# Routed experts of a Perceiver block: blocks of 64 places in pairs, weights of the fixed blocks loaded ahead

## The chip, the cores and the metric

The kernel runs on one core of a Trainium2 chip. The metric is the device time of one execution in microseconds (us). The core has TensorE (PE in the profile, with its weight loads as PEld), VectorE (DVE), ScalarE (ACT), GpSimd (POOL) and SyncE (SP), and 16 DMA engines that all queues share. SBUF has 128 partitions. PSUM has 8 banks of 512 f32 words per partition.

## The reference, cut to what matters

Six residual sub-layers follow one another on 8 x 64 = 512 tokens of width 256. Five are untouched in what they compute: cross attention, a delta-rule memory, a dense sum of 8 gated experts, a grouped cross attention, and a self attention (called stage e below). The sixth is a mixture of experts in which each token takes one expert:

```python
def _L1_ffn_ref(x, Wr, br, W1, b1, W2, b2):
    xf = x.reshape(-1, D)                       # 512 tokens x 256, already layer-normed
    logits = xf @ Wr.T + br                     # 8 experts
    expert_idx = jnp.argmax(logits, axis=-1)
    h = relu(einsum('td,efd->etf', xf, W1) + b1[:, None, :])      # 1024 wide
    y = einsum('etf,edf->etd', h, W2) + b2[:, None, :]
    out = y[expert_idx, arange(512)]
```

How many tokens an expert gets is known only at run time.

## The kernel before, in words

Each engine has its own program, written out by hand. They meet at semaphores only. The order of the work on an engine is the order of its lines.

**Router.** After stage e, `xn_tok` holds the normed tokens (partition = token). PE turns them round (`tr_pe`), waits for the two small arrays of the router (`in_wrt`, `wrt` and `b2f`, which SP loads at L474 to L476 once `x_tok` is complete), and makes the logits (L1057). DVE finds the first maximum and a one-hot `oh8` (L1790 to L1797). PE counts, with matrices of ones, the rank of each token within its expert and the total of each expert (L1065 to L1068). DVE then computes how many blocks each expert needs, where they begin (`starts`), which expert owns each block (`owner`, as row numbers `rows` of the weight array `wf`) and the `place` of each token (L1802 to L1821). In the meantime PE runs matmuls that nobody reads (`warm`, L334).

**Blocks of 128 places.** An expert with n tokens gets ceil(n / 128) blocks, and with 512 tokens and 8 experts there are at most NB = 11. All 11 are always run. For block k:

- *gather* (L1082): 16 one-pass matmuls with the one-hot `pick` (made by DVE, L1825) bring the tokens of the block into PSUM, features on partitions. ACT copies them to `xg` (L1394).
- *up* (L1104): 8 chunks of W1 x 2 halves of the width, each 128x128 weights against 128 places, full f32. The trace shows each such f32 matmul as two instructions, so 32 of them.
- ACT adds the bias and the relu for chunks 0 to 3 (L1408), DVE for chunks 4 to 7 (L1845).
- *down* (L1115): 8 matmuls (16 instructions) of `hb` against the 256 columns of W2, into bank 5.
- ACT and DVE split the result in a high and a low part (`yb_h` L1399, `yb_l` L1836), and *scatter* (L1093) adds it to the tokens in banks 6 and 7 with 8 matmuls against the one-hot `pickT` (L1830).

PE's order in step k is: up(k), scatter(k-1), gather(k+1), down(k). Steps 0 to 2, 9 and 10 are written out, 3 to 8 run in a loop of 3 steps.

**Weights.** One block needs 4104 words per partition, 2.1 MB (`ROW1`). POOL fetches them for every block by index, after `rows` is known (L574), into three buffers used in turn. The fetch for block k waits for down(k-3).

**SP's queue** holds all the direct loads in one order. Before the router come `wqkv` and `wproj` for stage e, then SP waits for `x_tok` and loads `wrt` and `b2f`.

Of the kernel before, what the change touches and what calls it, by code (L numbers as in the profile page):

```python
# [21 lines left out]
NB = NT + NEXP - 1  # L22
# [10 lines left out]
def const_layout():  # L33
# [18 lines left out]
        "column": np.broadcast_to(c, (P, P)),  # L52
        "row": p,
        "full": np.broadcast_to(P * np.arange(NT), (P, NT)),
        "before": np.broadcast_to((P * (c8.T > c8)).reshape(1, -1), (P, NEXP * NEXP)),
        "upto": np.broadcast_to((P * (c8.T >= c8)).reshape(1, -1), (P, NEXP * NEXP)),
        "block": np.broadcast_to(P * np.arange(NB), (P, NB)),
        "slot": p + P * np.arange(NB),
    }
# [63 lines left out]
def perceiver(nc, A, out):  # L123
# [13 lines left out]
    xn_tok = sb("xn_tok", NT, D)  # L137
    y_tok = sb("y_tok", NT, D)
    tmp_tok = sb("tmp_tok", NT, D)
    xnT = sb("xnT", KC, TOK)  # L140
    aT = sb("aT", KC, TOK)
# [4 lines left out]

    xnT_h = nc.alloc_sbuf_tensor("xnT_h", [P, KC, TOK], F32R)
    xnT_l = nc.alloc_sbuf_tensor("xnT_l", [P, KC, TOK], F32R)
# [112 lines left out]
    Ze = ce(NT, H, S)  # L261
    PT = ce(NT, H // 2, P)
    mxe, rie = ce(NT, H), ce(KC, TOK)
    assert ce.at <= after_wo1
    ce = Carve(after_wo1)
    wqkv, wproj = ce(KC, 3 * D), ce(KC, D)
    ce.at = after_wo1 + 2 * KC * FF
    vpair = ce(B, H // 2, 2, DK)
    assert ce.at <= after_ub

    cf = Carve()
    wblk = cf(3, ROW1)
    wf1 = [wblk[:, j, 0:KC * FF].rearrange("p (k n) -> p k n", k=KC) for j in range(3)]
    wf2 = [wblk[:, j, KC * FF:KC * FF + FC * D].rearrange("p (k n) -> p k n", k=FC) for j in range(3)]
    bf1 = [wblk[:, j, KC * FF + FC * D:] for j in range(3)]
# [3 lines left out]
    ohT8 = cf(TOK)  # L279
    over, blocks8 = cf(NEXP, NT), cf(NEXP)  # L280
    ends3, ends, starts3, starts = cf(NEXP, NEXP), cf(NEXP), cf(NEXP, NEXP), cf(NEXP)
    ended, owner, owner_row = cf(NB, NEXP), cf(NB), cf(NB)
    place3, place = cf(NT, NEXP), cf(NT)
    rel_place = cf(NB, NT)
    placed = cf(NT, P)
    placeT = cf(TOK)
    xg = cf(KC, P)
    hb = cf(FC, P)
    xn_h, xn_l = carve_r(cf, "xn_h", NT, D), carve_r(cf, "xn_l", NT, D)
    pick = carve_r(cf, "pick", 3, NT, P)  # L290
    pickT = carve_r(cf, "pickT", 3, TOK)
    yb_h, yb_l = carve_r(cf, "yb_h", D), carve_r(cf, "yb_l", D)
    rows = nc.alloc_sbuf_tensor_at("rows", [P, NB], mybir.dt.int32, offset=arena_base + 4 * cf.at)
    cf(NB)
# [100 lines left out]
    with nc.Block() as block:  # L395
# [3 lines left out]
        def _(sp):  # L399
# [73 lines left out]
            w_in(wproj, A["wproj"], "in_wqkv")  # L473
            sp.wait_ge(sem("x_tok"), 5)  # L474
# [8 lines left out]
        def _(pool):  # L483
# [72 lines left out]
            pool.memset(vpair, 0.0).then_inc(sem("e_set"), 1)  # L556
# [13 lines left out]
            pool.wait_ge(sem("f_rows"), 1)  # L570
            for k in range(NB):
                if k >= 3:
                    pool.wait_ge(sem("f_dn"), k - 2)
                pool.indirect_dma_start(wblk[:, k % 3, :], None, A["wf"],  # L574
                                        bass.IndirectOffsetOnAxis(ap=rows[:, k:k + 1], axis=0))\
                    .then_inc(sem(f"f_w{k % 3}"), 16)
# [3 lines left out]
        def _(pe):  # L580
# [429 lines left out]
            def weighted(t):  # L1010
# [8 lines left out]
                for kc in range(KC):  # L1019
                    for b2 in range(2):  # L1020
                        b = 2 * t + b2
                        for j in range(4):
                            last = pe.matmul(PS[32 * j:32 * j + 32, 2 * (t // 2), at(kc) + b2 * S:at(kc) + (b2 + 1) * S],
                                             vpair[:, b, 4 * kc + j].rearrange("p h d -> p (h d)"),
                                             PT[:, t, 2 * j + kc, b2 * S:(b2 + 1) * S], start=True, stop=True)
# [35 lines left out]
            pe.wait_ge(sem("f_oh8"), 1)  # L1061
# [11 lines left out]
            last.then_inc(sem("f_oht"), 1)  # L1073
            warm(pe, 7, 10)

            def gather(k, j):

                pe.wait_ge(sem("f_pick"), k + 1)
                for kc in range(KC):
                    for t in range(NT):  # L1080
                        for part in (xn_h, xn_l):
                            last = pe.matmul(PS[:, 0, kc * P:(kc + 1) * P], part[:, t, kc * P:(kc + 1) * P],  # L1082
                                             pick[:, j, t, :], start=t == 0 and part is xn_h,
                                             stop=t == NT - 1 and part is xn_l)
                last.then_inc(sem("f_x"), 1)

            def scatter(k, j, last_block=False):

                pe.wait_ge(sem("f_yl"), k + 1)
                pe.wait_ge(sem("f_pickT"), k + 1)  # L1090
                for t in range(NT):
                    for part in (yb_h, yb_l):
                        last = pe.matmul(PS[:, 6 + t // 2, (t % 2) * D:(t % 2 + 1) * D],  # L1093
                                         pickT[:, j, t * P:(t + 1) * P], part[:], start=False,
                                         stop=last_block and t % 2 == 1 and part is yb_l)
                return last

            def step(i, j, first=False, last_step=False):
                k = i * 3 + j
                pe.wait_ge(sem(f"f_w{j}"), i * 16 + 16)  # L1100
                pe.wait_ge(sem("f_xg"), k + 1)
                for c in range(FC):
                    for ki in range(KC):
                        last = pe.matmul(PS[:, 1 + c // 4, (c % 4) * P:(c % 4 + 1) * P],  # L1104
                                         wf1[j][:, ki, c * P:(c + 1) * P], xg[:, ki, :],
                                         start=ki == 0, stop=ki == KC - 1)
                    if c % 4 == 3:
                        last.then_inc(sem("f_upd" if c // 4 else "f_upa"), 1)
                if not first:
                    scatter(k - 1, (j + 2) % 3)  # L1110
                if not last_step:
                    gather(k + 1, (j + 1) % 3)
                for c in range(FC):
                    pe.wait_ge(sem("f_hd" if c // 4 else "f_ha"), k * 4 + c % 4 + 1)
                    last = pe.matmul(PS[:, 5, 0:D], hb[:, c, :], wf2[j][:, c, :], start=c == 0, stop=c == FC - 1)  # L1115
                last.then_inc(sem("f_dn"), 1)

            pe.wait_ge(sem("f_xnl"), 1)
            gather(0, 0)
            pe.wait_ge(sem("f_placed"), 1)  # L1120
            pe.matmul(bank(4), C("ones"), placed.rearrange("p a b -> p (a b)"), start=True, stop=True)\
              .then_inc(sem("f_place"), 1)
            pe.wait_ge(sem("f_ohs"), 1)
# [3 lines left out]
            step(0, 0, first=True)  # L1127
            step(0, 1)
            step(0, 2)
            with pe.Fori(1, NB // 3) as i:  # L1130
                for j in range(3):
                    step(i, j)
            step(NB // 3, 0)
            step(NB // 3, 1, last_step=True)
            scatter(NB - 1, 1, last_block=True).then_inc(sem("f_done"), 1)
# [3 lines left out]
        def _(act):  # L1139
# [220 lines left out]
            act.wait_ge(sem("e_set"), 1)  # L1360
            for n in range(2):
                act.wait_ge(sem("e_v"), n + 1)
                act.copy(vpair[0:S, 4 * n:4 * n + 4, :, 0, :],
# [6 lines left out]
            def turned(t):  # L1370
# [16 lines left out]
            act.copy(xn_h[:].rearrange("p a b -> p (a b)"), xn_tok[:].rearrange("p a b -> p (a b)"))\  # L1387
               .then_inc(sem("f_xnh"), 1)
            act.wait_ge(sem("f_oht"), 1)
            act.copy(ohT8[0:NEXP], PS[0:NEXP, 3, :]).then_inc(sem("f_ohs"), 1)  # L1390

            def tokens(k):
# [528 lines left out]
```

## Time and profile before

| | us |
|---|---|
| median of 3 runs | 948.43 (943.84 to 950.6) |
| the profiled execution's own time | 948.45 |
| its span on the core | 946.6 |
| start of the logits (L1057) | 816.20 |
| start of up(0) (L1104) | 833.20 |
| one block, start of up to start of the next up | 9.77 |
| split of the last result (L1399) | 939.82 |

The span counts from the first to the last instruction of the core. The routed part begins with the logits and ends with the store of the output at the end of the span. The page of the profile gives engine shares over the whole span, so what a change in this part is worth has to be read from the rows of this part.

### The profile page before, as it was taken

How to read it: one execution, taken by the hardware profiler on the slowest of the kernel's cores; microseconds unless marked ns; L12 is line 12 of the kernel's file. 1: busy time of each engine (PE TensorE's matmuls, PEld its weight loads, DVE VectorE, ACT ScalarE, POOL GpSimd, SP SyncE). 2: the span in 40 equal slices, each digit the busy share in tenths (PEclk: the TensorE clock that was granted, in tenths of full speed). 3: DMA queues.
4: the chain of work that ended last, by engine and by line, in shares of the span. 5: the costliest groups of instructions: out<-in, count | busy, mean ns of one | idle time of the engine just before them, and what ended most of it. 6: DMA issues, size and time to landing. Idle time of an engine off the chain costs nothing.

```text
span 946.6 us, 19810 instructions
## 1 busy us (share of the span) xinstructions
PE 886.3 (94%) x7764; PEld 748.1 (79%) x7764; DVE 513.6 (54%) x1168; ACT 414.6 (44%) x814; POOL 109.6 (12%) x105
## 2 busy tenths in 40 slices
PE   5998999999798899999999999999899997989997
PEld 3887887878666888888888888873799566789997
DVE  4776887777617555555555555543465246622322
ACT  3765666656622125444444444424466315111111
POOL 2323332130000700000000000000110012101000
PEclk9999999999999899999999999999899998999999
DMA  8544665454450000330331130054267000175650
GB/s 305 188 161 153 217 222 189 162 186 141 158 221 1 4 3 1 134 134 1 134 134 62 71 133 0 0 190 165 75 240 262 2 1 2 38 317 190 238 197 23
DMA packets 25286, 119.58 MB, mean 126 GB/s; under 512 B 2296, under 2 KB 8208, under 8 KB 21648
## 3 DMA queue, kind: packets, MB, share of 16 engines
q1 hardware_dynamic: 23472, 94.63, 27.2%
q0 software_dynamic: 1760, 24.17, 6.7%
q8 instruction: 41, 0.67, 0.3%
q14 instruction: 13, 0.11, 0.0%
HBM read 118.27 MB, written 0.52 MB: 125 GB/s over the span
## 4 chain that ended last, share of the span: by engine, by line
PE 80%; DVE 8%; DMA 6%; issue 2%; ACT 2%; SPq 1%; POOL 0%; DVEq 0%; ACTq 0%
PE PS L368 12%; PE PS L369 12%; PE PS L370 12%; DMA arena<-in_bias 4%; PE PS L1104 4%; PE PS L1115 4%; PE PS L377 4%; PE PS L664 4%; PE PS L906 3%; PE PS L787 3%; PE PS L925 3%; PE PS L653 2%; PE PS L676 2%; PE PS L1082 2%; PE PS L894 2%
## 5 line engine op out<-in xcount | busy, mean ns | idle before, releaser
L1646 DVE TENSOR_TENSOR w_l<-arena,w_h 128x768 fp32r<-128x768 f32 x64 | 61.2, 957 | 91.6 <-ACT w_h L1276 91.6
L1276 ACT CAST w_h<-arena 128x768 fp32r<-128x768 f32 x64 | 53.4, 836 | 129.2 <-PE PS L370 129.2
L368 PE MATMUL PS<-xnT_h,w_h 128*128 128x512 f32 x256 | 100.5, 393 | 0.8 <-DVE xnT_l L362 0.8
L369 PE MATMUL PS<-xnT_l,w_h 128*128 128x512 f32 x256 | 100.4, 392 | 0.0
L1484 DVE CUSTOM_DVE_ANT_0 arena<-PS,arena 128x512 f32<-128x512 f32 x128 | 87.0, 715 | 24.0 <-PE PS L653 17.9
L370 PE MATMUL PS<-xnT_h,w_l 128*128 128x512 f32 x256 | 99.6, 389 | 0.0
L1176 ACT ACTIVATE arena<-arena 128x1024 f32<-128x1024 f32 x64 | 73.5, 1150 | 11.1 <-DVE arena L1484 11.0
L370 PE MATMUL PS<-w_h,h_l 128*128 128x256 f32 x256 | 72.4, 283 | 0.0
L369 PE MATMUL PS<-w_l,h_h 128*128 128x256 f32 x256 | 72.4, 283 | 0.0
L368 PE MATMUL PS<-w_h,h_h 128*128 128x256 f32 x256 | 72.1, 282 | 0.0
L664 PE MATMUL PS<-consts,arena 128*128 128x128 f32 x512 | 69.1, 279 | 0.7 <-ACT arena L1181 0.4
L664 PEld LDWEIGHTS PS<-consts,arena 128*128 128x128 f32 x512 | 56.6, 142 | 10.9 <-issue 4.2
L1653 DVE TENSOR_TENSOR arena<-PS,arena 128x512 f32<-128x512 f32 x64 | 44.3, 692 | 30.5 <-PE PS L370 28.7
L370 PEld LDWEIGHTS PS<-xnT_h,w_l 128*128 128x128 f32 x256 | 48.1, 188 | 10.4
L368 PEld LDWEIGHTS PS<-xnT_h,w_h 128*128 128x128 f32 x256 | 48.3, 189 | 9.6 <-DVE xnT_l L362 1.2
L369 PEld LDWEIGHTS PS<-xnT_l,w_h 128*128 128x128 f32 x256 | 48.3, 189 | 7.7
L1491 DVE COPY arena<-PS 128x512 f32<-128x512 f32 x64 | 44.0, 687 | 17.0 <-PE PS L664 14.6
L1181 ACT COPY arena<-PS 128x512 f32<-128x512 f32 x64 | 37.2, 584 | 31.6 <-PE PS L664 31.6
L368 PEld LDWEIGHTS PS<-w_h,h_h 128*128 128x128 f32 x256 | 48.9, 191 | 2.4
L369 PEld LDWEIGHTS PS<-w_l,h_h 128*128 128x128 f32 x256 | 48.9, 191 | 2.4
L370 PEld LDWEIGHTS PS<-w_h,h_l 128*128 128x128 f32 x256 | 48.9, 191 | 0.0
L544 POOL COPY tmp_tok<-arena 128x1024 f32 (+1 forms) x4 | 4.2, 1042 | 359.8 <-ACT arena L1313 338.3
(284 smaller groups left out, 1943.1 us busy)
## 6 DMA issues: line engine op xcount, KB each, us to landing
arena<-in_bias SPq DMA_DIRECT2D x64, 512.0 KB, 4.7
arena<-in_wall SPq DMA_DIRECT2D x8, 3072.0 KB, 10.2
hT<-in_ctxT SPq DMA_DIRECT2D x12, 1024.0 KB, 6.8
arena<-in_ctxT SPq DMA_DIRECT2D x4, 1024.0 KB, 6.4
arena<-in_ctxG SPq DMA_DIRECT2D x4, 1024.0 KB, 4.9
hT<-in_ctxG SPq DMA_DIRECT2D x4, 1024.0 KB, 5.5
arena<-in_w SPq DMA_DIRECT2D x2, 1024.0 KB, 6.3
vecs<-in_vecs POOLq DMA_DIRECT2D x1, 1024.0 KB, 5.1
```

Source lines behind the costliest of these rows:

```text
L368: pe.matmul(out, a[0], b[0], start=start, stop=False)
L369: pe.matmul(out, a[0], b[1], start=False, stop=False)
L370: return pe.matmul(out, a[1], b[0], start=False, stop=stop)
L377: last = pe.matmul(PS[:, b0 + t // 2, (t % 2) * D:(t % 2) * D + n], lhsT[:, k, t * P:(t + 1) * P], rhs[:, k, 0:n], start=k == 0, stop=k == ...
L664: last = pe.transpose(PS[:, n, c * P:(c + 1) * P], ring[:, u, (4 * g + c) * P:(4 * g + c + 1) * P], C("ident"))
L1104: last = pe.matmul(PS[:, 1 + c // 4, (c % 4) * P:(c % 4 + 1) * P], wf1[j][:, ki, c * P:(c + 1) * P], xg[:, ki, :], start=ki == 0, stop=ki ...
L1176: act.activation(ring[:, u, :], ring[:, u, :], ACT.Exp, bias=nmax0[:, 1, u:u + 1], scale=-1.0, accum_out=rsum0[:, u:u + 1]).then_inc(sem(" ...
L1276: act.copy(w_h[:, s % 4, :], stage[s // 8 % 2][:, s % 8, :]).then_inc(sem("c_wh"), 1)
L1484: dve.tensor_tensor_reduce(out=ring[:, u, c], in0=bank(j), in1=ring[:, u, c], scale=-1.0, scalar=nmax0[:, 0, u:u + 1] if half else 3e38, o ...
L1491: dve.tensor_copy(pT[:, u % 4, 0:4, :].rearrange("p a b -> p (a b)"), bank(tile_bank("T", u, 0)))\
L1646: dve.tensor_tensor(w_l[:, s % 4, :], stage[s // 8 % 2][:, s % 8, :], wide(w_h[:, s % 4, :]), ALU.subtract).then_inc(sem("c_wl"), 1)
L1653: dve.tensor_tensor(hm[:, s % 2, :], bank(2 + s % 2), sg[:, s % 2, :], ALU.mult)\
```

## The change

**Blocks of 64 places.** Every expert gets one fixed block of 64 places. The tokens of rank 64 and above go to overflow blocks of 64. Seven of these suffice (`OVER`), and all seven are always run. Blocks are taken in pairs: pairs 0 to 3 are the fixed blocks (experts 0 and 1, 2 and 3, ...), pairs 4 to 6 are overflow blocks 0 to 5, and pair 7 is overflow block 6 alone. So there are 8 passes over PE in place of 11.

**PE per pair.** up has, for each of the two blocks, chunks x width halves x *two column halves of 64 weights*, each against 64 places: 64 matmuls, 128 instructions in the trace's count. down has 8 chunks x 2 blocks, 64 weights against 256 columns, where block 0 writes PSUM partitions 0 to 63 and block 1 writes 64 to 127. One scatter serves both blocks. One gather of 256 places serves two pairs, so there are 4 in place of 11.

**DVE and ACT per pair.** 8 relu instructions of 64 places each on either engine, where there were 4 of 128. The router's chain on DVE is reordered: the place of a token in a fixed block needs only its rank, so `picks(0)` and `picks(1)` are made ahead of the counting of overflow blocks. They are now 1024 words wide in place of 512. Five `warm` pairs replace ten.

**Weights.** SP loads the 8 fixed blocks ahead, each with a home of its own in SBUF. The overflow blocks are still fetched by index by POOL, one pair after each of the first four downs. To make room, buffers of stage e move (`Ze` to `hT`, `rie` to `tmp_tok`, `vpair` to `xnT_h` and `xnT_l` in two parts, with two memsets).

**Constants** grow from 1485 to 1617 words per partition.

On SP, at the end of the program, stood (names: out <- in, shape):

```order
L404 DMA arena<-in_wqkv 128x2x768 [waits d_u1,d_u0]
L404 DMA arena<-in_wproj 128x2x256
L404 DMA arena<-in_wrt 128x2x8 [waits x_tok]
L476 DMA arena<-in_b2f 8x256
L478 DMA out<-x_tok 128x4x256 [waits x_tok]
```

and now:

```order
L423 DMA arena<-in_wqkv 128x2x768 [waits d_u1,d_u0]
L423 DMA arena<-in_wproj 128x2x256
L495 DMA arena<-in_wf 128x4104 [waits d_w]
L495 DMA arena<-in_wf 128x4104 x2
L495 DMA arena<-in_wf 128x4104 [waits d_o]
L495 DMA arena<-in_wf 128x4104
L495 DMA arena<-in_wf 128x4104 [waits d_out]
L495 DMA arena<-in_wf 128x4104 [waits e_out]
L495 DMA arena<-in_wf 128x4104
L423 DMA arena<-in_wrt 128x2x8 [waits x_tok]
L510 DMA arena<-in_b2f 8x256
L512 DMA out<-x_tok 128x4x256 [waits x_tok]
```

Eight loads of 2.1 MB stand ahead of `wrt` and `b2f`, the last two of them released by the same stage (`e_out`) that completes `x_tok`.

On PE, the next to last step stood as

```order
L1104 MATMUL PS<-arena 128x128 [waits f_xg,f_w0]
L1104 MATMUL PS<-arena 128x128 x15
L1093 MATMUL PS<-yb_h,pickT 128x256 [waits f_pickT,f_yl]
L1093 MATMUL PS<-yb_l,pickT 128x256
...
L1082 MATMUL PS<-pick,xn_h 128x128 [waits f_pick]
...
L1115 MATMUL PS<-arena 128x256 [waits f_ha] x4
L1115 MATMUL PS<-arena 128x256 [waits f_hd] x4
```

and a pair without a gather now stands as

```order
L1142 MATMUL PS<-hT,arena 64x64 [waits f_xg,f_o2]
L1142 MATMUL PS<-hT,arena 64x64 x63
L1127 MATMUL PS<-yb_h,pickT 128x256 [waits f_pickT,f_yl]
L1127 MATMUL PS<-yb_l,pickT 128x256
...
L1154 MATMUL PS<-arena,hT 64x256 [waits f_ha]
L1154 MATMUL PS<-arena,hT 64x256
```

where the shapes are those of the output: up went from 16 matmuls of 128x128 to 64 of 64x64, and down from 8 of 128x256 to 16 of 64x256 (two rows of it are shown).

The diff, cut to its core:

```diff
-NB = NT + NEXP - 1
+BLK = 64
+OVER = TOK // BLK - 1
+PAIRS = NEXP // 2 + (OVER + 1) // 2
...
+            def expert_in(e):
+                sp.dma_start(wblk[e], A["wf"][e * P:(e + 1) * P]).then_inc(sem(f"f_w{e // 2}"), 16)
+
+            sp.wait_ge(sem("d_w"), 4 * B + 5)
+            for e in (0, 1, 2):
+                expert_in(e)
+            sp.wait_ge(sem("d_o"), FC)
+            for e in (3, 4):
+                expert_in(e)
+            sp.wait_ge(sem("d_out"), 2)
+            expert_in(5)
+            sp.wait_ge(sem("e_out"), 2)
+            for e in (6, 7):
+                expert_in(e)
             sp.wait_ge(sem("x_tok"), 5)
             w_in(wrt, A["wrt"], "in_wrt")
...
-            pool.wait_ge(sem("f_rows"), 1)
-            for k in range(NB):
-                if k >= 3:
-                    pool.wait_ge(sem("f_dn"), k - 2)
...
+            pool.wait_ge(sem("f_routed"), 4)
+            for o in range(OVER):
+                pool.wait_ge(sem("f_dn"), o // 2 + 1)
+                pool.indirect_dma_start(wblk[o], None, A["wf"],
+                                        bass.IndirectOffsetOnAxis(ap=rows[:, o:o + 1], axis=0))\
+                    .then_inc(sem(f"f_o{o // 2}"), 16)
...
-            warm(pe, 7, 10)
+            warm(pe, 7, 5)
...
+            def up(p, blocks):
+                pe.wait_ge(sem(f"f_w{p}" if p < 4 else f"f_o{p - 4}"), 16 * len(blocks))
+                pe.wait_ge(sem("f_xg"), p // 2 + 1)
                 for c in range(FC):
+                    for n, e in enumerate(blocks):
+                        tok = slice((p % 2) * P + n * BLK, (p % 2) * P + (n + 1) * BLK)
+                        at = n * 4 * BLK + (c % 4) * BLK
+                        for ki in range(KC):
+                            for r in halves:
+                                last = pe.matmul(PS[r, 1 + c // 4, at:at + BLK],
+                                                 wf1[e][:, ki, c * P + r.start:c * P + r.stop], xg[:, ki, tok],
+                                                 start=ki == 0, stop=ki == KC - 1)
...
+            def down(p, blocks):
+                if len(blocks) == 2:
+                    for c in range(FC):
+                        pe.wait_ge(sem("f_hd" if c // 4 else "f_ha"), 8 * p + 2 * (c % 4) + 2)
+                        for n, e in enumerate(blocks):
+                            last = pe.matmul(PS[halves[n], 5, 0:D], hb[:, c, n * BLK:(n + 1) * BLK], wf2[e][:, c, :],
+                                             start=c == 0, stop=c == FC - 1)
...
+            for p in range(PAIRS):
+                blocks = [e for e in (p % 4 * 2, p % 4 * 2 + 1) if p < 4 or e < OVER]
+                up(p, blocks)
+                if p == 0:
+                    pe.wait_ge(sem("f_routed"), 3)
+                    pe.matmul(bank(4), C("ones"), placed.rearrange("p a b -> p (a b)"), start=True, stop=True)\
+                      .then_inc(sem("f_place"), 1)
+                else:
+                    scatter(p - 1)
+                if p % 2 and p < PAIRS - 1:
+                    gather(p // 2 + 1)
+                down(p, blocks)
+            scatter(PAIRS - 1, last_pair=True).then_inc(sem("f_done"), 1)
...
             dve.wait_ge(sem("f_count"), 1)
+            ch.step(dve.tensor_tensor(rank3, PS[:, 4, 0:NT * NEXP].rearrange("p (t e) -> p t e", t=NT), oh8, ALU.mult))
+            ch.step(dve.reduce_sum(rank, rank3, axis=AX.X))
+            ch.step(dve.tensor_scalar(beyond, rank, float(BLK), None, ALU.is_ge))
+            ch.step(dve.tensor_tensor(first_place, rank, base, ALU.add))
+            ch.step(dve.scalar_tensor_tensor(rel_place[:, 0], beyond, 4096.0, first_place, ALU.mult, ALU.add))
...
+            picks(0, rel_place[:, 0])
+            ch.step(dve.tensor_scalar_add(rel_place[:, 1], rel_place[:, 0], -2.0 * P))
+            picks(1, rel_place[:, 1])
```

## Rows read from the trace of the kernel before

**Rows 1.** The page: busy time of the engines over the span

```profile
PE 886.3 (94%) x7764; PEld 748.1 (79%) x7764; DVE 513.6 (54%) x1168; ACT 414.6 (44%) x814; POOL 109.6 (12%) x105
```

**Rows 2.** Waits from 811 us on: engine line <- releaser: us, times, longest

```profile
DVE arena L1845 <- PE PS L1104: 40.4, 11, 12.4
PE PS L1104 <- DMA arena<-in_wf,rows: 2.7, 1, 2.7
```

**Rows 3.** Timeline, PE, blocks 0 to 2: start, us, line, shape, count

```profile
833.20 5.47 PE L1104 MATMUL PS<-arena 128*128 128x128 f32 x32 [2.66 <-DMA arena<-in_wf,rows]
...
843.74 3.73 PE L1104 MATMUL PS<-arena 128*128 128x128 f32 x32
847.23 0.36 PE L1093 MATMUL PS<-yb_h,pickT 128*128 128x256 f32 x1
...
848.26 0.22 PE L1082 MATMUL PS<-pick,xn_h 128*128 128x128 f32 x1
...
850.00 3.67 PE L1115 MATMUL PS<-arena 128*128 128x256 f32 x16
853.51 3.73 PE L1104 MATMUL PS<-arena 128*128 128x128 f32 x32
```

**Rows 4.** Timeline, ACT, the last split of a result

```profile
939.82 0.37 ACT L1399 CAST yb_h<-PS 128x256 fp32r<-128x256 f32 x1 [4.99 <-PE PS L1115]
```

**Rows 5.** Timeline, PE, router: start, us, line, shape, count

```profile
816.20 1.93 PE L1057 MATMUL PS<-arena,xnT 128*128 128x8 f32 x16
817.98 1.97 PE L334 MATMUL PS<-consts 128*128 128x256 f32 x8
827.54 1.07 PE L1121 MATMUL PS<-arena,consts 128*128 128x512 f32 x2
828.54 1.99 PE L1125 MATMUL PS<-arena 8*128 8x256 f32 x8
```

**Rows 6.** Timeline, PE, matmuls on parts of the array, all stages

```profile
796.55 0.63 PE L1023 MATMUL PS<-arena 128*32 128x64 f32 x32
304.89 2.09 PE L778 MATMUL PS<-arena 64*64 64x64 f32 x128 [1.26 <-DVE arena L1607]
313.06 27.11 PE L787 MATMUL PS<-arena 64*64 64x64 f32 x848 [0.80 <-DVE arena L1616]
781.01 3.71 PE L972 MATMUL PS<-arena,xnT 128*64 128x128 f32 x64
```

**Rows 7.** DMA issues: queue, KB each, median us to landing (x3: 811 to 833)

```profile
arena<-in_wall SPq DMA_DIRECT2D x8, 3072.0 KB, 10.2
arena<-in_ww SPq DMA_DIRECT2D x1, 256.0 KB, 7.8
out<-x_tok SPq DMA_DIRECT2D x1, 512.0 KB, 2.9
arena<-in_wf,rows POOLq DMA_INDIRECT x3, 13.3
```

**Rows 8.** Timeline: end of stage e on PE, then SP's issues

```profile
809.00 1.99 PE L1044 MATMUL PS<-arena,aT 128*128 128x256 f32 x8 [1.69 <-DVE aT L1769]
812.60 0.37 SPq L404 DMA_DIRECT2D arena<-in_wrt  x1
```

**Rows 9.** A stretch, PE alone: its us, busy, PEclk, DMA share, GB/s

```profile
833.20:838.40 5.20, 5.20 (x32) 0.67 0.89 369
```

**Rows 10.** Timeline, DVE, router to first pick

```profile
821.23 0.19 DVE L1802 TENSOR_TENSOR arena<-PS,consts 128x32 f32<-128x32 f32 x1 [0.62 <-PE PS L1068]
824.49 0.69 DVE L1825 TENSOR_TENSOR pick<-consts,arena 128x512 fp32r<-128x512 f32 x1
```

**Rows 11.** Groups on DVE and ACT: shapes, count | busy us, mean ns

```profile
L1466 DVE TENSOR_SCALAR arena<-PS,consts 128x64 f32<-128x64 f32 x16 | 4.5, 281 | 7.0 <-PE PS L681 7.0
L1799 DVE TENSOR_TENSOR xn_l<-xn_tok,xn_h 128x1024 fp32r<-128x1024 f32 x1 | 1.2, 1215 | 0.0
L1408 ACT ACTIVATE arena<-PS,arena 128x128 f32<-128x128 f32 x44 | 12.6, 369 | 22.3 <-PE PS L1104 22.3
```

More of the change, by code:

```diff
@@ L1093, in scatter @@
                         last = pe.matmul(PS[:, 6 + t // 2, (t % 2) * D:(t % 2 + 1) * D],
[L1094 to L1101 removed]
+                                         pickT[:, p % 2, t * P:(t + 1) * P], part[:], start=False,
@@ L1102, in step @@
+                                         stop=last_pair and t % 2 == 1 and part is yb_l)
+                return last
+            def up(p, blocks):
+                pe.wait_ge(sem(f"f_w{p}" if p < 4 else f"f_o{p - 4}"), 16 * len(blocks))
+                pe.wait_ge(sem("f_xg"), p // 2 + 1)
                 for c in range(FC):
[L1103 to L1106, printed above, removed]
+                    for n, e in enumerate(blocks):
[6 more added lines that the diff above has]
+                                                 start=ki == 0, stop=ki == KC - 1)
@@ L1107, in step @@
                     if c % 4 == 3:
                         last.then_inc(sem("f_upd" if c // 4 else "f_upa"), 1)
[L1109 to L1115, printed above, removed]
@@ L1116, in step @@
-                last.then_inc(sem("f_dn"), 1)
[L1118 to L1123, printed above, removed]
+            def down(p, blocks):
[6 more added lines that the diff above has]
+                else:
+                    for c in range(FC):
+                        pe.wait_ge(sem("f_hd" if c // 4 else "f_ha"), 8 * p + c % 4 + 1)
+                        last = pe.matmul(PS[halves[c % 2], 5, 0:D], hb[:, c, 0:BLK], wf2[blocks[0]][:, c, :],
+                                         start=c < 2, stop=c >= FC - 2)
+                last.then_inc(sem("f_dn"), 1)
@@ L1126, in _ @@
                           b2f[0:NEXP], start=t % 2 == 0, stop=False)
[L1127 to L1135, printed above, removed]
+            for p in range(PAIRS):
[5 more added lines that the diff above has]
+                      .then_inc(sem("f_place"), 1)
+                else:
+                    scatter(p - 1)
[3 more added lines that the diff above has]
+            scatter(PAIRS - 1, last_pair=True).then_inc(sem("f_done"), 1)
         @block.scalar
@@ L1401, in step @@
-            def step(i, j, first=False, last_step=False):
-                k = i * 3 + j
-                if not first:
-                    result(k - 1)
-                act.wait_ge(sem(f"f_w{j}"), i * 16 + 16)
-                act.wait_ge(sem("f_upa"), k + 1)
-                for c in range(4):
-                    act.activation(hb[:, c, :], PS[:, 1, c * P:(c + 1) * P], ACT.Relu, bias=bf1[j][:, c:c + 1])\
-                       .then_inc(sem("f_ha"), 1)
-                if not last_step:
-                    tokens(k + 1)
@@ L1413, in _ @@
-            tokens(0)
-            act.wait_ge(sem("f_place"), 1)
-            act.copy(placeT, bank(4)).then_inc(sem("f_placeT"), 1)
-            step(0, 0, first=True)
-            step(0, 1)
-            step(0, 2)
-            with act.Fori(1, NB // 3) as i:
-                for j in range(3):
-                    step(i, j)
-            step(NB // 3, 0)
-            step(NB // 3, 1, last_step=True)
-            result(NB - 1)
+            act.copy(xn_h, xn_tok[:]).then_inc(sem("f_xnh"), 1)
```

225 lines of the change are left out of this document (122 added, 103 removed).

## The prediction, made before the changed kernel was run

> **What bounds the kernel now.** I read the page first. Its shares say that PE is busy for 94% of the span [rows 1], but they average over six stages, and only the last is changed. The list of waits from 811 us on comes next. In it PE waits once for weights, 2.7 us ahead of block 0, and DVE waits for PE in all 11 blocks, 40.4 us in sum [rows 2]. Fetching weights is hidden in every block but the first, so loading them ahead can give back those 2.7 us and little more. The timeline of PE shows what a block is made of: up 3.49 (843.74 to 847.23), scatter 1.03 (to 848.26), gather 1.74 (to 850.00), down 3.51 (to 853.51), in all 9.77 with no gap [rows 3]. From the first up to the split of the last result pass 939.82 - 833.20 = 106.6 us [rows 3, 4]. This part is bound by PE, and what counts is how many PE passes there are and what one costs.
>
> **The pair loop.** 11 passes become 7 of two blocks and one of a single block.
>
> - *up.* The same half of W1 now goes in as two column halves of 64 weights against 64 places. That is 128 instructions per pair and 64 in the last, 960 in all. No row has full-height weights of 64 columns against 64 columns. From below: 32 instructions in 3.49 us are 109 ns for 128 columns on the whole array [rows 3], so half the columns with two halves at work at once would be 27 ns. From above, if 64 columns cost what 128 do, the row of column halves with 128 columns has 3.71 / 64 = 58 ns [rows 6]. Nearest are the products of stage two, 64x64 weights against 64 columns on two tiles in turn: 27.11 / 848 = 32 ns, and with four tiles 2.09 / 128 = 16 ns, that is 33 for each two [rows 6]. They have the same width of weights and of stream, so I take 32: 960 x 0.032 = 30.7 us. The ends are 26 and 56 us.
> - *down.* Two blocks side by side on the halves, 32 instructions of 256 columns. They take what 16 on the full array took, 3.51 [rows 3], since L972 shows two halves at half the pitch of a full-width matmul (58 against 109 ns) [rows 3, 6]. 7 x 3.51 + 1.75 for the single block = 26.3.
> - *scatter*, 7 inside the loop at 1.03 = 7.2 [rows 3].
> - *gather*, 3 inside the loop. Each has 16 one-pass matmuls of 256 columns, and the scatter has 8 such in 1.03 [rows 3], so 2.06 each, 6.2.
> - the count of places (L1121), which moves from ahead of block 0 to behind up(0): 1.0 [rows 5].
>
> The loop is 30.7 + 26.3 + 7.2 + 6.2 + 1.0 = 71.4 against 106.6, so 35.2 less.
>
> **What hides the rest of a pair.** DVE has 8 relu instructions of 64 places. A read of 64 words from PSUM took 281 ns, overlapped with the next [rows 11], so 8 are at most 2.2 us. They begin when up ends, and PE first has scatter (1.03) and the half of down that ACT feeds (1.75). The last chunk is needed 1.03 + 3.1 us after up. ACT's eight, at most 0.369 us each [rows 11], begin at half of up and must be there for the first part of down; 2.0 + 1.03 us stand ahead of their need, the later ones have more. If this cover went, about 1 us per pair would come back. The split of a result runs under the next up, as now. The longer picks (1.2 us for 1024 words [rows 11]) follow the relus, with a down still ahead.
>
> **Overflow weights.** POOL fetches two blocks after each of the first downs. Three fetches issued back to back landed after 13.3 us in the median [rows 7]. Between a fetch and the up that needs it lie three whole pairs each time (the fetch behind pair 0 serves pair 4, and so on), 28 us or more by the terms above. I cost them at nothing. At twice the landing time they would still be there.
>
> **The start, if nothing else moved.** DVE needed 3.26 us and 15 small steps from the counts (821.23) to the first pick (824.49), 0.22 each [rows 10]. Now 5 steps stand ahead of it: pick from 822.3, 1.2 us long [rows 11], gather from 823.7 for 2.06, the eight matmuls of b2 for 2.0 [rows 5], up(0) at 827.8. ACT copies the tokens under those eight. That is 5.4 earlier than 833.20 [rows 3]. Two more steps ahead of `xn_l` end by 821.1, before the counts are there.
>
> **What is queued ahead of the router's arrays.** This is the wait that I expect in place of the one removed. SP now issues experts 6 and 7 when stage e's last product is done, 809.00 + 1.99 = 811.0, and `wrt` only behind them, in the same queue [rows 8]. They are 4.2 MB. A load of 3.15 MB took 10.2 us from issue to landing, one of 0.52 MB took 2.9 [rows 7]: 7.3 us for 2.6 MB, 2.8 per MB. So 4.2 MB land 2.9 + 3.7 x 2.8 = 13.2 after 811.1, at 824.3. Does a small load wait for large ones ahead of it? `ww`, 256 KB behind two of 1 MB, took 7.8 us where 512 KB alone took 2.9 [rows 7]. I take it as held back until 824.4. PE wanted it at 816.20 [rows 5], so 8.2 us are lost.
>
> In those 8 us PE stands still. After a gap of 2.66 us the first up of block 0 ran at a granted clock of 0.67, mostly the lower level of 1.2 GHz, and took 5.2 us in place of 3.49 [rows 3, 9]. The logits, 1.8 us at the full 2.4 GHz [rows 5], should take 1.8 more. The delay is 8.2 + 1.8 = 10.0, and up(0) starts at 837.8, that is 4.6 later than before.
>
> The earlier loads (experts 0 to 5, from 738 us on) have nothing behind them that is wanted; `wqkv` is issued ahead of them. The memsets and moved buffers of stage e keep their number of words. The larger constants (68 KB more, 0.2 us by the same rate) lie under the first layer norm.
>
> **Sum.** Span 946.6 + 4.6 - 35.2 = 916.0. The profiled execution took 1.85 us more than its span, so 917.9. It stood at 948.45 against a median of 948.43, so nothing is to be corrected.
>
> **Where a rule speaks against this.** One row shows column tiles at work together: 32 instructions with 32 weight columns each and all 128 rows, four column groups in turn, took 0.63 us, under 20 ns each [rows 6], where one full-height matmul of 8 columns takes 1.78 / 16 = 111 ns [rows 5]. So loads of weights into one column group run while another group, over the same rows, works. The Trainium skill, "TensorE: Matmul & The Clock Gate", Part 3, The mechanism, says that a weight load overlaps with matmuls in flight only when the row group differs. By it the two halves of up, which share all rows, would load and stream one after the other, and the sum would be that of the third rival below. The trace speaks against it here.
>
> **Rivals.**
>
> 1. *The router's arrays aren't held back.* Small transfers could slip through between the large ones. For it: the landing of `ww` could be slow for its own layout. Against: 7.8 us. The 10.0 us fall away: 908.
> 2. *64 columns cost what 128 do.* The column-half row has only 128 and 512 columns to show. up is then 960 x 0.058 = 55.7, 25 us more: 943. Against: the 32 ns of the products [rows 6], but those use half the rows of the array.
> 3. *The halves take turns (slower than before).* In up each instruction then loads 64 columns and streams 64 alone: half of 111 [rows 5] and half of 107 to 109 [rows 3] make 109 ns. up is 960 x 0.109 = 104.6 in place of 30.7, 74 more: 992. The point from which it decides is the pitch of up: at 32 + 30.6 / 0.96 = 64 ns the change is worth nothing. Against: the 20 ns and the 58 ns [rows 6].
> 4. *PE is held up for another reason in each pair*, by its instructions (256 of them in 4 us, where the products had as many in 8), or by ACT and DVE at 64 places. At 1 us per pair 926, at 2 us 934.
> 5. *The preload does nothing, or the blocks aren't halved at run time*: the loop has fixed counts, so only the 2.7 us of rows 2 are open, and these are in the sum.
>
> **Numbers.** My case has 0.62 (between 913, with 27 ns, and 923), rival 1 0.14, rival 2 0.07, rival 3 0.05, rival 4 0.12. The time is 918. The range 903 to 932 takes in the first case, rival 1 with its own lower pitch, and most of rival 4, and leaves out about 0.15. A measurement of this kernel can tell about 1% (9.5 us) from no change. Rivals 2 and 3 end outside "faster": 943 is within 1%, 992 is slower. Hence faster 0.89, same 0.06, slower 0.05.
>
> **What the new profile would show.** The logits start near 824.4 behind a PE idle time ended by the DMA of `wrt`, not near 816. Experts 6 and 7 land at about 824. The matmuls of up (128*64, 128x64) have a pitch of 32 ns, a pair's up 4.1 us. A pair without a gather lasts 8.6 us, one with it 10.7, the last 4.9. up(0) starts near 838, the last split is near 909. No PE wait for `wf` at pairs 4 to 7. I am wrong if the logits start near 816, if up has a pitch of 50 ns or more, or if a wait of over 1 us stands ahead of down in every pair.

## The result and the profile after

The changed kernel takes **919.62 us** (median of 4 runs, 916.57 to 922.94), the kernel before 947.82 (943.84 to 950.6): ratio 0.9715 (the plain quotient of the two medians is 0.9702), 95% interval 0.9682 to 0.9747. A later set gave 917.93 against 945.11, ratio 0.9712 (0.9684 to 0.9740). The forecast was 918.

The span fell from 946.6 to 918.2, by 28.4 us. The profile cuts this into three pieces, at SP's issue of `wrt` and at the start of the first up:

| piece | before | after | difference | forecast |
|---|---|---|---|---|
| start to issue of `wrt` | 812.60 | 807.78 | -4.8 | 0 |
| issue of `wrt` to up(0) | 20.6 | 29.0 | +8.4 | +4.6 |
| up(0) to the last split | 106.6 | 74.5 | -32.1 | -35.2 |

The pieces before are from [rows 3, 4, 8]. So the total is closer than its terms, and that is luck: two terms were too good by 3.8 and 3.1 us, and 4.8 us that nobody forecast made up for most of it.

The page of the kernel after, busy time of the engines, answers to [rows 1]. PE has 526 more instructions and is busy for 30.5 us less:

```profile
PE 855.8 (93%) x8290; PEld 709.5 (77%) x8290; DVE 508.3 (55%) x1182; ACT 412.6 (45%) x820; POOL 105.6 (12%) x102
```

The list of waits of the kernel after, from 811 us on, answers to [rows 2]. A line has engine, name and line, the releaser, then us in sum, times, longest:

```profile
DVE hT L1885 <- PE PS L1142: 27.5, 8, 4.4
...
PE PS L1091 <- DMA arena<-in_b2f: 8.0, 1, 8.0
PEld PS L1142 <- issue: 3.5, 9, 0.5
...
PE PS L1142 <- issue: 2.1, 6, 0.4
```

PE's old wait for `wf` is gone and no wait for weights is left. Two things are new: 8.0 us for the router's arrays, and short stops of PE inside up whose releaser is "issue", that is nothing that the profile shows.

Timeline of PE after, router to first up (start, us, line, shape, count), against [rows 5]:

```profile
819.56 3.55 PE L1091 MATMUL PS<-arena,xnT 128*128 128x8 f32 x16 [8.02 <-DMA arena<-in_b2f]
822.96 3.76 PE L353 MATMUL PS<-consts 128*128 128x256 f32 x8
826.51 0.49 PE L1099 MATMUL PS<-consts,small 128*128 128x40 f32 x2
...
829.74 3.34 PE L353 MATMUL PS<-consts 128*128 128x256 f32 x10
...
834.89 1.99 PE L1167 MATMUL PS<-arena,hT 8*128 8x256 f32 x8
836.81 3.95 PE L1142 MATMUL PS<-hT,arena 128*64 128x64 f32 x128
```

Stretches of the same engine (us, busy and count, PEclk, DMA share, GB/s): the logits, the first and the second group of the matmuls that are only there to keep PE at work (L353, "warm" below), then up of pairs 1, 2 and 5:

```profile
819.50:822.90 3.40, 3.34 (x16) 0.50 0.00 0
822.90:826.50 3.60, 3.60 (x9) 0.50 0.02 5
829.70:832.70 3.00, 3.00 (x11) 0.65 0.00 0
845.25:850.50 5.25, 4.54 (x131) 1.00 0.49 141
857.03:862.27 5.24, 4.51 (x130) 1.00 0.93 354
887.44:891.27 3.83, 3.83 (x130) 1.00 0.14 56
```

The granted clock is 0.50, that is 1.2 GHz, from the logits through the first warm group. And up lasts 3.83 us at full clock where nothing stops it, 30 ns per instruction, but 5.25 in pairs 1 to 3, at full clock too. The first of these in the timeline of PE:

```profile
845.25 2.75 PE L1142 MATMUL PS<-hT,arena 128*64 128x64 f32 x79
848.34 0.39 PE L1142 MATMUL PS<-hT,arena 128*64 128x64 f32 x6 [0.34 <-issue]
849.07 1.50 PE L1142 MATMUL PS<-hT,arena 128*64 128x64 f32 x43 [0.34 <-issue]
```

The timeline of POOL has in the same stretch its two indexed fetches (L608), and two more in the next up:

```profile
846.31 1.04 POOL L608 DMA_INDIRECT arena<-in_wf,rows  x1 [62.81 <-PE PS L1154]
847.65 0.97 POOL L608 DMA_INDIRECT arena<-in_wf,rows  x1 [0.31 <-issue]
857.48 0.94 POOL L608 DMA_INDIRECT arena<-in_wf,rows  x1 [8.86 <-PE PS L1154]
858.73 0.94 POOL L608 DMA_INDIRECT arena<-in_wf,rows  x1 [0.30 <-issue]
```

In pairs 1, 2 and 3 alike the two stops of PE begin 0.35 to 0.43 us and 1.08 to 1.17 us behind the start of POOL's second fetch (the rows shown are those of pair 1; the others are alike). The stops are 0.7 us of the 1.4 by which such an up is longer; in the rest PE counts as busy (4.5 us instead of 3.83), so the matmuls beside the stops are slower too.

Three questions follow: is the router late because of the two loads ahead of its arrays, and of nothing else; what stops PE in up; and do the column halves carry the gain of the loop.

### The profile page after: what moved, and what is told of

Same layout as the page of the kernel before. It is cut to its first block, busy times and chain, and to the rows that moved or that the text cites. A ratio compares the mean times of both kernels' runs of the same rounds, so it can differ in the third digit from the quotient of the medians.

```text
span 918.2 us, 20804 instructions
## 1 busy us (share of the span) xinstructions
PE 855.8 (93%) x8290; PEld 709.5 (77%) x8290; DVE 508.3 (55%) x1182; ACT 412.6 (45%) x820; POOL 105.6 (12%) x102
## 4 chain that ended last, share of the span: by engine, by line
PE 85%; DVE 7%; DMA 3%; issue 2%; ACT 2%; SPq 0%; DVEq 0%; ACTq 0%
PE PS L387 13%; PE PS L388 13%; PE PS L389 13%; PE PS L698 5%; PE PS L396 4%; PE PS L940 4%; PE PS L1142 3%; PE PS L821 3%; PE PS L959 3%; PE PS L710 3%; PE PS L687 3%; PE PS L1154 3%; DMA arena<-in_bias 2%; PE PS L928 2%; PE PS L913 2%
```

## The experiments

In the expectations, "ahead" means in front in SP's queue, and the issue of `wrt` serves as the zero, because what stands ahead of it moves by a few us from kernel to kernel.

### 1. The router's arrays first

```
+            sp.wait_ge(sem("x_tok"), 5)
+            w_in(wrt, A["wrt"], "in_wrt")
+            sp.dma_start(b2f[0:NEXP], ...)
             sp.wait_ge(sem("e_out"), 2)
             for e in (6, 7): expert_in(e)
-            (the same three lines, from here)
```

> SP issues wrt and b2f ahead of experts 6 and 7, nothing else changes. Theory H (the router's arrays were held back behind 4.2 MB in SP's queue): the logits start 8.0 us earlier, right behind the turned tokens, PE never stands still there, so the logits, the warm matmuls and the counts run at the full clock too. In the trace of the change these took 13.2 us from the start of the logits to the first gather, against 9.4 before; at the full clock and with the shorter chain 7.5 are left. So 8.0 + 5.7 = 13.7 us less, a time near 906 and an up(0) some 22.5 to 23.5 us behind the issue of wrt less 8 us, that is about 15 us behind it. Rival (only the 8.0 us of standing still were lost, the slow clock cost nothing on the path): 911 to 912. Rival (the small arrays were late for another reason, their own layout): no change, 919 to 920.

904.13 us (901.56 to 907.7), ratio to before 0.9554 (0.9493 to 0.9616). SP's issues and PE's start in the router:

```profile
803.29 0.38 SPq L423 DMA_DIRECT2D arena<-in_wrt  x1
803.71 0.41 SPq L507 DMA_DIRECT2D arena<-in_b2f  x1
804.18 0.82 SPq L495 DMA_DIRECT2D arena<-in_wf  x2
```

```profile
806.89 1.93 PE L1091 MATMUL PS<-arena,xnT 128*128 128x8 f32 x16
818.33 3.95 PE L1142 MATMUL PS<-hT,arena 128*64 128x64 f32 x128
```

The logits start 3.60 us behind the issue of `wrt`, as before the change, with no wait; up(0) starts 15.0 behind it instead of 29.0. The 14.0 us are both parts: 8.2 of waiting and 5.8 that the idle PE cost afterwards, since logits to up(0) now take 11.44 us in place of 17.25, at a granted clock of 1.00 throughout. The medians differ by 15.5 us; the rows explain 14.0 of them. up in pairs 1 to 3 stays at 5.22 to 5.23, so that stop has another cause.

### 2. The loads that hold the arrays back, put into the kernel before

```
+            sp.wait_ge(sem("e_out"), 2)
+            for n in range(2):   # two blocks of 2.1 MB, into words free by then
+                sp.dma_start(arena[...], A["wf"][...])
             sp.wait_ge(sem("x_tok"), 5)
             w_in(wrt, A["wrt"], "in_wrt")
```

> The kernel before, with one thing added: two loads of 2.1 MB each into unused words of SBUF, issued at the end of stage e ahead of wrt and b2f in SP's queue. Theory H (queueing alone holds the router back, and the slow clock behind it costs as much again): the logits start 8 us later than in the kernel before, and the first gather 8 + 3.7 to 5.7 = 12 to 14 us later. Block 0 then starts about 12 to 13 us later (its clock is full this time, its weights come 9 us behind the rows as before), up(0) may take 3.5 in place of 5.2 if the router's work keeps the clock up. In all 10 to 14 us slower than before, 957 to 962. Rival (the small arrays are late in the changed kernel for its own reasons): no change, 947 to 948.

961.93 us (958.04 to 963.15), ratio 1.0176 (1.0117 to 1.0235). The router's rows:

```profile
821.50 3.56 PE L1062 MATMUL PS<-arena,xnT 128*128 128x8 f32 x16 [7.89 <-DMA arena<-in_b2f]
...
842.75 5.46 PE L1109 MATMUL PS<-arena 128*128 128x128 f32 x32 [0.99 <-DMA arena<-in_wf,rows]
```

`wrt` was issued at 809.85, so the logits are 11.65 behind it and not 3.60, and the first up 32.9 and not 20.6. The cause is the same from the other side: the two loads alone cost 12.3 us from the issue of `wrt` to the first up, 8.05 as a later start of the logits and 4.25 behind it, where the clock was 0.50 from 821.5 to 832. The interval of the ratio reaches from 1.2% to 2.4%, so the size is read from these rows. One part of the expectation failed: up(0) takes 5.2 us as before, and not 3.5, although PE stood still for only 0.99 us ahead of it.

### 3. No warm matmuls in the router

```
-            warm(pe, 7, 4)
...
-            warm(pe, 7, 5)
```

> The changed kernel without the two groups of matmuls that nobody reads between the logits and the first gather (8 and 10 instructions). In the trace of the change the clock was at its lower level from the logits to the transposes, and the groups took 3.55 and 2.99 us. Theory W (at the lower clock these groups are longer than the work of DVE that they cover, so the counts began 2.0 us after the one-hot was there, and the gather 1.3 us after the pick): the path from the logits to the gather shrinks from 13.2 to about 10 us, a gain of 3.3. Rival (without them the clock stays low for longer, and gather, the b2 matmuls and up(0) take up to twice as long, 4.1 and 3.9 us more): a loss of 1 to 5 us.

923.07 us (1 run; the slowest of the four runs of the change had 922.94, so the time alone says nothing and the rows decide). The first warm group keeps PE past the moment at which the counts could start (in the kernel after, DVE has the one-hot table ready at 824.45, and PE gets to L1099 at 826.51). Without it, logits to gather take 10.14 us in place of 13.17. But the clock stays low for longer:

```profile
830.30:833.90 3.60, 3.60 (x16) 0.50 0.00 0
837.65:843.40 5.75, 5.75 (x129) 0.63 0.01 3
```

The first row is the gather (3.68 in whole, 2.16 in the kernel after), the second up(0) (5.76 against 3.88), and b2 between them took 3.71 against 1.92. These are 5.2 us for the 3.0 gained, so leaving the warm matmuls out loses some 2 us. Once PE has stood still, they make the path longer and what follows shorter, and the two nearly cancel. What helps is not to stand still, as in experiment 1.

### 4. No fetch of overflow weights

POOL's loop of fetches is left out, and pairs 4 to 7 wait for the weights of the fixed blocks (`f_w{p % 4}`), so overflow blocks compute with stale weights.

```
-            for o in range(OVER):
-                pool.wait_ge(sem("f_dn"), o // 2 + 1)
-                pool.indirect_dma_start(wblk[o], ...)
...
-                pe.wait_ge(sem(f"f_w{p}" if p < 4 else f"f_o{p - 4}"), 16 * len(blocks))
+                pe.wait_ge(sem(f"f_w{p % 4}"), 32)
(the same wait changes on ACT and DVE)
```

> The seven fetches of overflow blocks by index are left out, and the overflow blocks use the weights that lie in the same buffers (so their results differ); all matmuls, waits between engines and picks stay. In the trace of the change the up of pairs 1, 2 and 3 took 5.25 us against 3.83 in pairs 5 and 6, with stretches in which PE waits for nothing but its own instructions; these are the pairs in which POOL issues two fetches and the DMA engines are busy. Theory F (the fetches, by POOL's work or by their traffic, delay the supply of PE's instructions): all up stages take 3.8 to 3.9 us, 4.2 + 0.3 us less in sum, a time near 915. Rival (the position in the program or the placement of the weights in SBUF is the cause): the up of pairs 1 to 3 stays at 5.25 and the time at 919 to 920.

913.26 us (912.4 to 914.57), ratio 0.9643 (0.9583 to 0.9703). up of pairs 1 to 3:

```profile
842.10:845.93 3.83, 3.83 (x131) 1.00 0.01 4
852.45:856.28 3.83, 3.83 (x131) 1.00 0.00 0
860.92:864.75 3.83, 3.83 (x130) 1.00 0.02 4
```

The fetches are what stops PE, 1.4 us for each two. The rows leave open by which of their two halves: the traffic, or POOL's work on the descriptors.

### 5. The same traffic without POOL

```
-                pool.indirect_dma_start(wblk[o], None, A["wf"], ...rows[:, o:o + 1]...)
+                sp.wait_ge(sem("f_dn"), o // 2 + 1)
+                sp.dma_start(wblk[o], A["wf"][o * P:(o + 1) * P])
```

Overflow blocks get the weights of experts 0, 1, ... here, at the same moments and of the same size.

> The overflow blocks are loaded by SP with direct loads of fixed experts at the same moments and of the same size, in place of POOL's fetches by index (so the results of overflow blocks differ). Traffic is the same, POOL does nothing. Theory F1 (the traffic on the DMA engines delays PE's instructions): the up of pairs 1 to 3 stays near 5.25 us. Theory F2 (POOL's making of descriptors for a fetch by index does it): up falls to 3.8 to 3.9 us in all pairs. Both only by the rows of up; the time itself should be 915 to 920.

up of pairs 1 to 3, with the DMA engines as busy as in the kernel after:

```profile
842.97:846.80 3.83, 3.83 (x130) 1.00 0.72 214
853.34:857.17 3.83, 3.83 (x131) 1.00 0.92 330
861.88:865.72 3.84, 3.84 (x131) 1.00 0.95 393
```

The time was 913.26 us (1 run), that of experiment 4. Traffic at a share of 0.95 costs nothing in these three; what costs is the indexed fetch issued by POOL while up runs. By what way POOL's issue reaches PE stays open. A late supply of PE's instructions is the reading of "issue", with 128 matmuls and as many weight loads in 3.83 us, but it isn't shown: in the DMA view of the kernel after, a packet of the queue "instruction" starts in the ups of pairs 1, 2, 4 and 5 and none in that of pair 3, while pairs 1 to 3 are stopped and pair 5 is not.

### 6. The fetches behind up, with the router first

Experiment 1, and POOL waits for the end of the next up instead of the end of a down:

```
-                pool.wait_ge(sem("f_dn"), o // 2 + 1)
+                pool.wait_ge(sem("f_upd"), o // 2 + 2)
```

> The router's arrays ahead of experts 6 and 7, and POOL's fetches by index wait for the end of up of the next pair in place of the end of down, so that POOL makes descriptors while PE does scatter and down, which have few instructions per us. Theory F2 (POOL's making of descriptors holds up PE only where PE needs many instructions): up takes 3.83 us in pairs 1 to 4, 1.4 x 3 + 0.3 = 4.5 us less than with the router's arrays first alone, a time near 900, and scatter and down stay at 1.0 to 1.1 and 3.5. The fetches come 4 to 5 us later and have 23 us left. Rival (POOL's descriptors cost PE the same time wherever they are made): the 1.4 us move to scatter or down, and the time stays at 904. Rival (later fetches land too late): a wait for weights at pair 5 or 6.

**899.24 us** (896.95 to 901.13), ratio 0.9506 (0.9448 to 0.9564), the fastest here. Against experiment 1 the intervals overlap; the rows decide. up of pairs 1, 2, 3 and 5:

```profile
828.73:832.57 3.84, 3.84 (x131) 1.00 0.02 4
839.08:842.91 3.83, 3.83 (x130) 1.00 0.97 407
847.55:851.39 3.84, 3.84 (x131) 1.00 0.93 376
866.38:870.90 4.52, 4.05 (x130) 1.00 0.99 418
```

POOL's fetches now lie beside scatter and down, which lose nothing (6.51 us from the end of up of pair 1 to the next up, 6.53 before), and no pair waits for weights. The traffic of these fetches still runs beside the ups of pairs 2 and 3, at a share of 0.97 and 0.93, and does not stop them: the stop goes with POOL's issuing. up(0) to the last split fell to 70.7 us. Pair 5 has one gap of 0.47 us at 870.52, 7 us behind POOL's last descriptors (issued from 862.11 on) and with the DMA share at 0.99. So traffic may cost a little once; I did not separate that.

### 7. up with weights over the full width

```
-                            for r in halves:
-                                pe.matmul(PS[r, ...], wf1[e][:, ki, c * P + r.start:c * P + r.stop], ...)
+                            pe.matmul(PS[:, ...], wf1[e][:, ki, c * P:(c + 1) * P], ...)
```

> The up matmuls take all 128 columns of a chunk at once against 64 places, as before the change, in place of two column halves: 32 instructions per block in place of 64, the rest of the change stays. Theory C (a full-width load costs about 110 ns however few columns are streamed, and the halves are what makes 64 places worth less than 128): up takes 64 x 0.110 = 7.0 us per pair in place of 3.9 (5.25 in pairs 1 to 3), and 3.5 in the last. That is 7 x 7.0 + 3.5 = 52.5 against 33.5, 19 us more, a time near 939. There are half as many instructions, so no stretches of waiting for instructions are expected. Rival (full-width matmuls of 64 columns cost half of those of 128): 64 x 0.055 = 3.5 us per pair, a time of 916 to 920, and the halves bring nothing.

946.29 us (938.28 to 951.0), ratio 0.9976 (0.9939 to 1.0013): no faster than before. Timeline of PE, up of pairs 0 and 2:

```profile
839.42 12.26 PE L1141 MATMUL PS<-hT,arena 128*128 128x64 f32 x64
...
871.52 7.36 PE L1141 MATMUL PS<-hT,arena 128*128 128x64 f32 x64
```

At full clock 64 instructions take 7.17 us, 112 ns each, about as with 128 columns (109). All ups sum to 58.7 us against 33.4 with halves. up(0) to the last split is 102.0 us: against 106.6 in the kernel before, the fewer passes still give 4.6 us, and by an estimate would give 9.5 if pair 0 took 7.17 like the others. The later start of up(0), 29.6 us behind the issue of `wrt` and not 20.6, takes this back, so that in the time nothing is left without the halves. Pair 0 was a surprise (below).

### 8. The halves one after the other

```
-   for each chunk, block, ki: a matmul on the lower half, then one on the upper
+   for four chunks: all matmuls on the lower half, then all on the upper
```

> The changed kernel, with the up matmuls of one column half grouped: 16 on the left half, then 16 on the right, in place of one on each in turn. Same instructions, same operands. Theory A (the halves work at the same time only where neighbouring matmuls are on different ones; each half has a pitch of 60 ns): up takes 128 x 0.060 = 7.7 us per pair in place of 3.85, 3.85 in the last pair, a time near 945. Theory B (a half is loaded and streamed with no overlap inside it): 128 x 0.109 = 14 us per pair, near 990. Rival (the order does not matter): 3.85 us per pair and 919 to 920.

934.11 us (1 run). Timeline of PE, up of pair 1:

```profile
856.99 7.09 PE L1143 MATMUL PS<-hT,arena 128*64 128x64 f32 x128
```

7.02 us to the next instruction, 55 ns each. The same 128 instructions take 30 ns each if they change halves every time. Within one half, load and stream together take 55 ns, and not the 109 of the third rival. But one full-width instruction does the work of two on halves, so the same work costs 112 ns at full width, 110 on halves in turn and 60 with the halves alternating: the order brings nearly all of the gain.

Experiments 7 and 8 also answer a question of experiments 4 and 5. They keep POOL's fetches, and yet up takes 7.17 and 7.02 us in pairs 1 to 3 as in pairs 5 and 6. In the kernel before, POOL fetches at 844.18, inside the second up, which takes 3.49 like the others. So the stop showed only at the pitch of 30 ns, and not at 55, 109 or 112.

### 9 to 12. Where do the 4.8 us ahead of the router come from?

They lie in the first stage: its end (SP's issue of `w1`, which waits for it) moved from 249.57 to 243.56 us, and the change there is only a larger array of constants and other code further on. The kernel before was run again for one profile:

> The kernel before, unchanged, for a second profile. If the end of the first stage is fixed by the program, it is near 249.6 us again; if it varies from run to run, it may lie anywhere from 242 to 250. The routed part from the issue of wrt on should repeat: up(0) 20.6 us behind it, 106.6 us from there to the last split.

947.55 us, first stage 248.24, `wrt` at 811.95, up(0) 20.4 behind it, 106.6 from there to the last split. Then the kernel before with 132 unused words more per constant row:

```
+        "unused": np.zeros((P, 132)),
```

> The kernel before, with the array of constants made 132 words longer per partition (1617, as in the changed kernel), by words that nobody reads. All later buffers move by 528 bytes, nothing else changes. In the traces so far the first stage (up to SP's load of w1_0), which the change does not touch, ended at 247.1 and 249.6 us in the two based on the kernel before and at 242.1 to 244.6 in the eight with the change. Theory S (the place of the buffers in SBUF costs or gives this): this kernel ends the first stage at 242 to 245, and its time is 3 to 5 us below the kernel before, 943. Rival (it varies from run to run, or comes from the longer program): the first stage ends at 246 to 250, and the time is 947 within the interval.

945.87 us (942.82 to 952.89), ratio 1.0001 (0.9973 to 1.0028). Its first stage ended at 244.99, near the changed kernel's, yet `wrt` was issued at 810.34, only 1.6 to 2.3 us earlier than in the two profiles of the kernel before, and the time did not move. Then the kernel before with its loop over blocks 3 to 8 written out on PE, ACT and DVE:

```
-            with pe.Fori(1, NB // 3) as i:
+            for i in range(1, NB // 3):
```

> The kernel before, with the loop over blocks 3 to 8 written out on PE, ACT and DVE, as the changed kernel has no loop there. The work is the same. Open is why some 5 us of the gain lie ahead of the router: the stages up to the issue of wrt took 807.8 us with the change against 812.0 and 812.6 before, and the larger constants alone gave nothing (ratio 1.0001). Theory P (the length and the loops of the program, by the place of the instructions or their supply, cost or give this): the first stage ends at 242 to 245 us, and the time is 3 to 5 us below the kernel before, near 943. Rival (it is something else): 947, within the interval.

942.79 us (938.63 to 945.87), ratio 0.9973 (0.9953 to 0.9993), some 2.5 us, with the first stage at 249.35; if this is a part, it is not the part that was sought. And the change once more:

> The changed kernel, unchanged, for a narrower interval and a second profile on the same chip. If the 4 to 5 us ahead of the router belong to the program, the issue of wrt is at 804 to 809 us again, the ratio to the kernel before stays at 0.970 to 0.973, and the time is 919 to 920. If they were chance, the ratio comes out near 0.975, 924. From the issue of wrt on: up(0) 29.0 us behind it, 74.5 from there to the last split, up of 5.25 us in pairs 1 to 3.

917.93 us; first stage 242.87, up(0) 29.3 behind `wrt`, up of pairs 1 to 3 5.32 to 5.33. In the profiles of all nine runs of kernels built from the change the first stage ends between 242.1 and 244.6; in four built from the kernel before between 247.1 and 249.6, in the one with larger constants at 245.0. So the shift is real, repeats, and **its cause stays open**. One lead: the 64 loads of `in_bias` in that stage land after 4.7 us in the median in the kernel before and after 4.1 in the kernel after. Whether that is a cause or a consequence no run here shows.

## Why the prediction was right, and where its terms were not

- **The loads in SP's queue.** Right in mechanism and size: 8.2 forecast; the logits are 11.78 us behind the issue of `wrt` in place of 3.60, so 8.2. A load of 8 KB waited for 4.2 MB ahead of it. Rival 1 is excluded, and experiment 1 shows what it would have given.
- **The start without the wait.** 11.6 us from logits to up(0) were forecast (827.8 - 816.2), and experiment 1 has 11.44.
- **What the stop leaves behind.** This is the term that was mis-sized most. The prediction charged the slow clock for the logits alone, 1.8 us. The kernel after needs 17.25 from logits to up(0), 5.8 more than with PE kept busy. The clock was at 0.50 until 829.7 and 0.65 on average until 832.7, and both warm groups (3.6 and 3.0 us, against 1.8 and 2.2 in experiment 1) held up what stood behind them. [rows 9] had shown a whole up of 5.2 us behind a gap of 2.66, which was a hint that more than the first instructions pay. That row is itself no clean price of a gap: in experiment 2 the same up takes 5.2 us behind a gap of 0.99, and in experiment 7 the clock falls in up(0) behind no gap at all.
- **up.** 30 ns per instruction against 32 from the products on 64x64 tiles, so 28.8 in place of 30.7 us for all 960 without a stop. Rivals 2 and 3 are excluded by this; experiments 7 and 8 show what they would rest on, 112 and 55 ns. The rule of the Trainium skill that the prediction weighed ("TensorE: Matmul & The Clock Gate", Part 3, The mechanism) would have the two halves load and stream in turn, since both use all rows. The pitch of 30 ns alternating against 55 ns in one half speaks against it for column halves, as [rows 6] did, and the measurement stands.
- **PE held up in each pair.** Rival 4, with a chance of 0.12 at 1 us or more per pair, came true in part: 1.4 us in pairs 1 to 3 and 0.3 in pair 4, 4.5 in all. The step "overflow fetches cost nothing" failed. It asked only when the weights would land; that was right, no pair waits for them. It did not ask what POOL's issue does to PE meanwhile. up is 33.4 in sum, 2.7 over its term; the rest of the loop is 41.2 against 40.7.
- **Relus, picks, splits** are hidden as forecast. PE waits 0.93 us for `yb_l` ahead of the last scatter, where no up follows that could cover the split; the kernel before waits 0.92 at the same place, so this is no cost of the change.
- **Ahead of the router** nothing was forecast and 4.8 us were gained, cause open. Without them the span would have been 923.0, 7 above the forecast 916.0. The range would still have held the time, but the forecast of 918 owes its nearness to them.

## What to carry over

Put a preload behind every small load that the same queue still owes to someone: the order of SP's lines was worth 14 us here, 8.2 as a wait and 5.8 because the waiting engine's clock was at half and its filler work came onto the path. Where, as here, f32 weights are wider (128) than the stream is long (64), try them as column halves and change halves with every matmul; grouped by half, nearly all of the gain was gone. And price an indexed fetch not by its landing alone, but ask what PE runs while POOL issues it: beside matmuls at a pitch of 30 ns two fetches cost 1.4 us and a single one 0.3, beside those at 55 ns and more nothing.

## What the runs showed of the hardware

- f32 weights over all 128 rows against 64 columns: 112 ns per instruction with 128 weight columns, 55 with 64 when 32 instructions in a row stay on one column half, 30 with the halves alternating (experiments 7 and 8 and the kernel after).
- Two indexed fetches issued by POOL (0.94 to 1.04 us each) lengthen an up with a pitch of 30 ns by 1.4 us; direct loads of the same size by SP do not, and ups with a pitch of 55 or 112 ns are not lengthened.
- PE's clock can fall although PE is never idle. Experiment 7, the stretch ahead of up(0), up(0) with full-width weights against 64 columns, and the same work in pair 2:

```profile
835.30:839.40 4.10, 4.10 (x26) 1.00 0.00 0
839.40:851.50 12.10, 12.10 (x66) 0.58 0.00 0
871.52:878.69 7.17, 7.17 (x67) 1.00 0.74 286
```

With halves the same stretch of pair 0 ran at 1.00 in 3.88 us. A busy share of 100% is no sign of the full clock.
